# Output products on 64 rows in turns, small products placed later, parts handed over by halves

## The chip, the cores and the metric

One core of one Trainium2 chip runs the whole program. The metric is the device time of one execution in microseconds. The kernel is written directly for the engines: TensorE (PE, with its weight loads as PEld), VectorE (DVE), ScalarE (ACT), GpSimd (POOL) and SyncE (SP), which issues the DMAs. Each engine has its own program, and they meet in semaphores.

## The reference

The input x is 16 samples of 128 channels, 32x32 pixels, f32. Four residual layers follow one another, each `x = x + layer(groupnorm(x))`, with a group norm over 4 channels:

- Layer 0: a convolution gives three maps (two offsets, one mask) for each pixel; the normalised image is sampled bilinearly there, and then comes a depthwise 3x3 and a pointwise convolution.
- Layer 1: the image is pooled 3x3; a 3x3 convolution of the pooled image gives 18 offsets and 9 masks; the pooled image is sampled at nine places for each pixel (deformable convolution) and multiplied with 9 x 128 x 128 weights.
- Layer 2: a dense 3x3 convolution with weights made from `weight` and `r_matrix`.
- Layer 3: a 1x1 projection to two halves of 64 channels. One goes through a small two-layer net (x_conv), the other through a horizontal and a vertical strip attention (attn). Both are gated, concatenated and go through the output projection:

```python
out = jnp.concatenate([spatial_map, channel_map], axis=1)   # 64 + 64 channels
return _pw(out, proj_out_w, proj_out_b)                      # 128 -> 128
```

## The kernel before

All is f32. A pass takes two samples, so there are eight passes: a loop of seven (`PASSES - 1`), in which the next pass's first layer is worked in, and a last one without it. In layers 0 to 2 a sample's 128 channels lie on the 128 partitions. In layer 3 the two samples share the partitions, 64 channels each (sample 0 on 0 to 63, sample 1 on 64 to 127). A call of matmul (`mm`) in f32 stands as two records in the trace, each with its weight load. A product of 512 columns is a half image of one sample.

The order of TensorE's work is written out by hand. `conv` (L516) makes a 3x3 convolution as 9 products for the upper half (h = 0) and 9 for the lower half (h = 1), and takes hooks: `hooks[h, k]` is called before product (h, k). In a pass TensorE does this:

1. Layer 1's offset parts of sample 0: `offset_parts(2, ...)` (L488), 18 products of 32 output columns in turns on four column groups, into the bank psO. ScalarE's `parts` (L932 is the copy that many helpers share) moves them to SBUF as two copies, one for each half of the image, and `offsets(i, 2, 27)` (L500) sums the four groups for each of 8 tiles, 16 records. VectorE adds the bias (L1528); TensorE doubles the result (`doubles`, L602); VectorE makes hat functions from it (`hats`, L1502 to L1514). Then the same parts for sample 1 (`offset_parts(3, ...)`), a far test, block transposes (L594), `offsets(i, 3, 27)`.
2. For each sample the sampling products (`near`, L627: 64 rows by 144 columns, in turns on two row groups), which ScalarE copies out, and layer 1's convolution from the samples (`conv(psO[0], w1, ...)`). In the second of these convolutions hooks hold, for the next pass: at (0, 3) layer 0's tap rows (`tap_rows`, L641), at (1, 3) layer 0's small offset products (`next_offsets`: `offsets(i + 1, 0, 6)`, L500, 16 records of 54 rows and 6 columns), and at (1, 6) the product of layer 0's far test (`start_far`, L649). Between rows and offsets the rows go to ScalarE (`rows`), through nine DMAs that shift them (SP, `move`), and back to ScalarE (`tap_tiles`, two copies).
3. Layer 2's convolution (`conv(psO[1], w2, ...)`, L516), with layer 0's block products of the next pass between its products (L558, L564, L576). Before that stands, at (0, 5), the group mean of "L2B" (L479).
4. Layer 3 in pieces (L847 to L866), with the next pass's pointwise and depthwise convolution (`conv0`, L720) as filling between them; at the end the output products (L901, L902): for sample s and half h one with the spatial map (`sm`, weights `woT[:, s, 0, :]`) and one with the channel map (`at`, weights `wo2[:, s, :]`), both over 128 rows. The weights have zeros on the other sample's 64 rows. The group mean of "L1B" stands before sample 1's second half.

VectorE's order in the same places: after layer 1's sampling it takes the convolution of each sample into x (L1612), makes statistics (L1225 to L1233), waits for the group mean, and makes the affine (L1246 to L1262; a step on GpSimd, L455, in between). For sample 1 it does, ahead of the wait for the convolution, the next pass's layer 0: the offsets' sum (`start_offsets`, L1332, L1299, L1303), the flag (`start_flag`, L1309, L1343) and seven steps of the hat functions of sample 0 (`start_hat`, L1352 to L1369). At the end of a pass it does: pooling of sample 0 (`pool3`, L1387 to L1393) with the residual of layer 0 in between (L1398), the variance of "L1B", the last residual of sample 0 (`store_ready`, L1737), the scale of "L1B" for ScalarE's normalisation (L954), pooling of sample 1, the last residual of sample 1.

## Time and profile before

| | |
|---|---|
| median of 3 runs | 1719.94 us (1717.85 to 1722.87) |
| the profiled execution | 1719.42 us, span 1717.6 us |
| TensorE busy | 1591.8 us, 93% of the span |
| VectorE, ScalarE busy | 66%, 38% |
| mean granted clock of TensorE | 0.958 |
| a pass in the loop | about 203 us |

A row of the timeline merges equal instructions that follow one another; its length runs from the first one's start to the last one's end, and the ends of matmuls are modelled. "idle [.. <- ..]" is how long the engine did nothing before it, and what ended that. A window's mean clock of 0.75 means that half of it was at 1.2 GHz.

### The profile page before, as it was taken

The numbers are of one execution on the slowest core, as the hardware profiler recorded it, in microseconds if no ns is written. First come the engines' busy times: TensorE is split into PE (matmuls) and PEld (weight loads), VectorE is DVE, ScalarE is ACT, GpSimd is POOL, SyncE is SP. The second block draws the span as 40 slices with busy tenths as digits, with TensorE's granted clock in tenths as the row PEclk, the third lists the DMA queues.
The fourth block names the chain that finished last, engine by engine and source line by source line (L and its number), as shares of the span: only waits on it lengthen the run. The fifth ranks groups of instructions, "written<-read, shape, count | busy, mean of one in ns | idle before, by whom it ended". The sixth has DMA issues, their size and how long they took to land.

```text
span 1717.6 us, 22494 instructions
## 1 busy us (share of the span) xinstructions
PE 1591.8 (93%) x7252; PEld 837.6 (49%) x7252; DVE 1141.4 (66%) x2139; ACT 659.3 (38%) x1066; POOL 50.2 (3%) x76
## 2 busy tenths in 40 slices
PE   2979999999999999999999999999999999999975
PEld 1537453565435554365534645355543655337422
DVE  4358349864598457883498835985469844887266
ACT  2126224461345413453244622555134541346131
POOL 2000000000000000000000000000000000000000
PEclk8989999999999999999999999999999999999987
DMA  3000000100001000000001000010000100000000
GB/s 117 14 13 2 7 1 1 51 5 4 1 1 52 7 2 1 26 27 7 1 1 51 2 6 1 1 52 7 2 1 14 39 7 2 1 25 2 1 0 25
DMA packets 7971, 24.61 MB, mean 14 GB/s; under 512 B 1664, under 2 KB 2368, under 8 KB 7792
## 3 DMA queue, kind: packets, MB, share of 16 engines
q1 hardware_dynamic: 7792, 22.40, 3.5%
q8 instruction: 91, 1.49, 0.4%
q14 instruction: 88, 0.72, 0.1%
HBM read 12.13 MB, written 8.39 MB: 12 GB/s over the span
## 4 chain that ended last, share of the span: by engine, by line
PE 75%; DVE 11%; issue 6%; ACT 4%; SPq 3%; DMA 1%; POOL 1%; DVEq 0%; POOLq 0%; ACTq 0%
PE psN L516 14%; PE psO L516 13%; PE psN L851 11%; PE psO L720 7%; PE psN L720 5%; PE psN L627 4%; PE psO L576 4%; SPq L414 3%; ACT samp L932 2%; DVE samp L1662 2%; PE psN L594 2%; PE psN L558 2%; PE psN L564 2%; PE psM L500 2%; PE psN L901 1%
## 5 line engine op out<-in xcount | busy, mean ns | idle before, releaser
L516 PE MATMUL psO<-samp,w 128*128 128x512 f32 x576 | 285.2, 631 | 0.0
L516 PE MATMUL psN<-xn,w 128*128 128x512 f32 x576 | 278.7, 605 | 1.7 <-DVE yout L1409 0.9
L1143 ACT ACTIVATE samp<-psN,vec 128x512 f32<-128x512 f32 x160 | 110.0, 687 | 130.4 <-PE psN L851 130.4
L516 PEld LDWEIGHTS psO<-samp,w 128*128 128x128 f32 x576 | 106.6, 200 | 102.6 <-issue 96.2
L1317 DVE COPY xblk<-psN 120x256 f32<-120x256 f32 x128 | 54.3, 424 | 142.7 <-PE psN L558 142.7
L932 ACT ACTIVATE samp<-psN 128x576 f32<-128x576 f32 x192 | 118.2, 676 | 58.1 <-PE psN L627 58.0
L516 PEld LDWEIGHTS psN<-xn,w 128*128 128x128 f32 x576 | 98.3, 189 | 84.5 <-issue 84.5
L932 ACT ACTIVATE G<-psN 120x256 f32<-120x256 f32 x128 | 49.1, 383 | 229.6 <-PE psN L564 229.6
L720 PE MATMUL psN<-img,w 128*128 128x512 f32 x288 | 133.4, 608 | 0.0
L720 PE MATMUL psO<-img,w 128*128 128x512 f32 x288 | 133.0, 603 | 0.0
L627 PE MATMUL psN<-GQt,xq 64*128 64x144 f32 x1536 | 123.1, 297 | 10.6 <-ACT samp L932 9.0
L627 PEld LDWEIGHTS psN<-GQt,xq 64*128 64x128 f32 x1536 | 103.3, 186 | 26.1 <-ACT samp L932 16.5
L954 ACT ACTIVATE xn<-x,gst 128x1024 f32<-128x1024 f32 x32 | 40.1, 1254 | 189.7 <-DVE gst L1262 189.7
L1587 DVE TENSOR_TENSOR GTs<-hf 128x576 f32<-128x576 f32 x128 | 95.7, 758 | 15.1 <-DVE flag L1309 11.8
L1598 DVE STREAM_TRANSPOSE GQt<-GTs 128x576 f32<-128x576 f32 x128 | 96.9, 767 | 3.9 <-PE psN L627 3.9
L455 POOL TENSOR_TENSOR gst<-gst,neg_half 128x1 f32<-128x1 f32 x64 | 42.4, 662 | 1588.7 <-DVE gst L1251 1588.7
L720 PEld LDWEIGHTS psO<-img,w 128*128 128x128 f32 x288 | 53.7, 188 | 68.4 <-issue 68.4
L851 PE MATMUL psN<-samp,kh_w 128*128 128x512 f32 x160 | 79.1, 636 | 8.3 <-DVE samp L1662 8.3
L720 PEld LDWEIGHTS psN<-img,w 128*128 128x128 f32 x288 | 51.9, 188 | 69.8 <-issue 69.8
L851 PE MATMUL psN<-samp,kv_w 128*128 128x512 f32 x160 | 78.6, 633 | 5.8 <-DVE samp L1662 5.8
L500 PE MATMUL psM<-tab,Gd 128*128 128x27 f32 (+1 forms) x384 | 51.8, 280 | 33.0 <-ACT Gd L932 33.0
L576 PE MATMUL psO<-G,xblk 120*128 120x128 f32 x512 | 79.7, 278 | 0.9
(156 smaller groups left out, 2299.9 us busy)
## 6 DMA issues: line engine op xcount, KB each, us to landing
xin<-in_x SPq DMA_DIRECT2D x16, 512.0 KB, 4.1
out<-yout SPq DMA_DIRECT2D x16, 512.0 KB, 3.7
pool_v<-rows SPq DMA_DIRECT2D x72, 25.5 KB
w<-in_w SPq DMA_DIRECT2D x2, 576.0 KB, 5.1
samp<-in_r SPq DMA_DIRECT2D x1, 576.0 KB, 6.8
tab<-in_tab SPq DMA_DIRECT2D x1, 513.0 KB, 5.3
kh_w<-in_kh SPq DMA_DIRECT2D x1, 320.0 KB, 5.4
kv_w<-in_kv SPq DMA_DIRECT2D x1, 320.0 KB, 5.6
```

The lines of the kernel that those rows point to most:

```text
L414: sp.dma_start(pool_v[k:k + ROWS - K9 + 1:K9].rearrange("p r c -> p (r c)"), rows[k:k + ROWS - K9 + 1:K9, first:first + H * EDGE])\
L500: last = mm(ps[s][:, 4 + m * t:4 + m * t + m], off_parts[s][0:used, C * t:C * t + C], table, start=True, stop=True)
L516: last = mm(dst[:, h, :], wgt[:, k, :], rhs(h, k), start=(k == 0), stop=(k == K9 - 1))
L576: last = mm(psO[0][:, p // 4, C * (p % 4):C * (p % 4) + C], xblk[p % 2][:, u, :], G1[p % 2][:, u, :], start=(u == 0), stop=(u == 1))
L627: last = mm(pair(s, u)[:, g, :].rearrange("p (k r c) -> p k r c", k=K9, c=SW)[:, :, :, cols], xQ[rows, t, a, e, :], w[rows, e, :, :, cols] ...
L720: ins = mm(dst[:, h, :], w0[:, k, :], window(img[s])(h, k), start=(k == 0), stop=(k == K9 - 1))
L851: mm(product(m), lhsT, rhs[:, HALF * h:HALF * h + HALF], start=True, stop=True)\
L932: return nc.scalar.activation(out, in_, ACT.Copy)
L1143: nc.scalar.activation(out, bank(m)[0:out.shape[0]], fn, **kw).then_inc(l3_act.sem, 1)
L1317: v_.tensor_copy(xblk[b][:].rearrange("p h c -> p (h c)"), psT[0:BLK, 1, 0:2 * C])\
L1587: v_.tensor_tensor(GQ[n % 2][:].rearrange("p (k a b) -> p k a b", a=QR, b=QB), hy[:, ORDER[n]].unsqueeze(3).broadcast_to((C, PAIRS * K9, Q ...
L1598: v_.transpose(GQt[o % RING][:].rearrange("p e k r c -> p (e k r c)"), GQ[(n - 1) % 2][:])\
```

## The change

Four edits:

- The output products are made on 64 rows each. For each half, first the spatial and then the channel map, and within these the two samples in turns, sample 0 on partitions 0 to 63 and sample 1 on 64 to 127. The four accumulations go to the same four banks as before. The wait for `added(i + 1, 1)` stands before all of them and the group mean of "L1B" behind all of them. Both samples' semaphore increments come in the last pair of products.
- `next_offsets` moves from (1, 3) to (1, 6), `start_far` from (1, 6) to (1, 8).
- `offset_parts` counts its semaphore once for each half, `parts` on ScalarE waits and counts for each half, and `offsets` takes the tiles of the upper half (0, 2, 4, 6) first and then waits for the lower half. `tap_tiles`, which also feeds `offsets`, still counts once.
- VectorE's seven steps `start_hat(own, i + 1, 0, part)` move from ahead of the wait for the second sample's convolution to behind its statistics, ahead of the affine of "L2B".

```diff
@@ offset_parts, in the loop over h
-                last.then_inc(parts_product.sem, 1)
+                    last.then_inc(parts_product.sem, 1)
@@ offsets
-                pe.wait_ge(parts_ready.sem, parts_ready.at(i, max(n, 1)))
-                for t in range(TILES):
+                for t in (0, 2, 4, 6, 1, 3, 5, 7):
+                    if t < 2:
+                        pe.wait_ge(parts_ready.sem, parts_ready.at(i, (1, 2 * n - 2 + t)[n > 0]))
@@ hooks of layer 1's second convolution
-                            hooks[1, 3] = next_offsets
-                            hooks[1, 6] = lambda: start_far(i + 1)
+                            hooks[1, 6] = next_offsets
+                            hooks[1, 8] = lambda: start_far(i + 1)
@@ layer 3's output products
-                for s in range(2):
-                    if s and more:
-                        pe.wait_ge(added.sem, added.at(i + 1, 1))
-                    for h in range(2):
-                        hh = slice(HALF * h, HALF * h + HALF)
-                        if h and more and s:
-                            group_mean(i, "L1B", order)
-                        mm(final[s][:, h, :], woT[:, s, 0, :], sm[:, hh], start=True, stop=False)
-                        last = mm(final[s][:, h, :], wo2[:, s, :], at[:, hh], start=False, stop=True)
-                    last.then_inc(l3_product.sem, 1)
+                if more:
+                    pe.wait_ge(added.sem, added.at(i + 1, 1))
+                for h in range(2):
+                    hh = slice(HALF * h, HALF * h + HALF)
+                    for m, weights, maps in ((0, woT[:, :, 0, :], sm), (1, wo2, at)):
+                        for s in range(2):
+                            own = slice(C2 * s, C2 * s + C2)
+                            last = mm(final[s][:, h, :], weights[own, s, :], maps[own, hh], start=(m == 0), stop=(m == 1))
+                            if h and m:
+                                last.then_inc(l3_product.sem, 1)
+                if more:
+                    group_mean(i, "L1B", order)
@@ parts, on ScalarE
-                act.wait_ge(parts_product.sem, parts_product.at(i, n - 1))
                 for b in range(2):
-                    last = copy(...)
-                last.then_inc(parts_ready.sem, 1)
+                    act.wait_ge(parts_product.sem, parts_product.at(i, 2 * n - 3 + b))
+                    copy(...).then_inc(parts_ready.sem, 1)
@@ VectorE, for sample s of layer 1
                     if s and more:
                         start_offsets(own, i + 1)
                         start_flag(own, i + 1)
-                        for part in range(START_HAT):
-                            start_hat(own, i + 1, 0, part)
 
                     dve.wait_ge(conv_ready.sem, conv_ready.at(i, 3 + s))
                     ...
                     stats(own, ("L2A", "L2B")[s], order)
+                    if s and more:
+                        for part in range(START_HAT):
+                            start_hat(own, i + 1, 0, part)
                     affine(own, ("L2A", "L2B")[s], order)
```

## Rows read from the trace of the kernel before

**Rows 1.** The page, part 1: busy us (share of the span) and instructions of each engine.

```profile
PE 1591.8 (93%) x7252; PEld 837.6 (49%) x7252; DVE 1141.4 (66%) x2139; ACT 659.3 (38%) x1066; POOL 50.2 (3%) x76
```

**Rows 2.** Timeline, 787 to 804 us: start, us, engine, line, operation, out<-in, count [idle before].

```profile
787.93 6.25 PE L516 MATMUL psO<-samp,w 128*128 128x512 f32 x14
...
794.89 1.15 ACT L932 ACTIVATE Gd<-pool_v 54x512 f32<-54x512 f32 x2 [3.83 <-DMA pool_v<-rows]
...
796.10 2.32 PE L500 MATMUL psM<-tab,Gd 54*128 54x6 f32 x16 [1.91 <-ACT Gd L932]
...
798.35 5.49 PE L516 MATMUL psO<-samp,w 128*128 128x512 f32 x6
...
803.63 0.42 PE L649 MATMUL psM<-flagf,tab 128*128 128x1 f32 x2
...
803.92 3.02 PE L516 MATMUL psO<-samp,w 128*128 128x512 f32 x6
```

**Rows 3.** Windows: length, busy us of PE, PEld, DVE, ACT, POOL, then PEclk, DMA.

```profile
183.98:196.69 12.71, 10.81 (x31) 6.48 (x31) 2.85 (x11) 1.46 (x4) 0.00 (x0) 0.73 0.01 2
...
sum 84.27, PE 70.89 PEld 40.43 DVE 20.32 ACT 10.21 POOL 0.00; mean PE 10.13 PEld 5.78 DVE 2.90 ACT 1.46 POOL 0.00
...
738.90:740.76 1.86, 1.86 (x20) 1.82 (x18) 1.83 (x4) 1.33 (x3) 0.00 (x0) 1.00 0.00 0
...
1704.00:1709.00 5.00, 5.00 (x7) 2.00 (x6) 0.00 (x0) 0.00 (x0) 0.00 (x0) 0.51 0.00 0
```

**Rows 4.** Timeline of layer 1's offset products, second sample.

```profile
738.89 1.87 PE L500 MATMUL psM<-tab,Gd 128*128 128x27 f32 x16
```

**Rows 5.** Timeline behind them, 804 to 818 us: VectorE, and TensorE's first block product.

```profile
804.35 0.19 DVE L1352 SCALAR_TENSOR_TENSOR om_start<-om_start,tab 128x32 f32<-128x32 f32 x1
...
807.10 0.42 DVE L1369 SCALAR_TENSOR_TENSOR hat<-hat,mk 128x256 f32<-128x256 f32 x1
...
812.95 0.21 DVE L1262 TENSOR_SCALAR gst<-gst 128x1 f32<-128x1 f32 x1
...
817.02 0.38 PE L558 MATMUL psN<-ident,strip 128*120 128x128 f32 x2
```

**Rows 6.** Timeline from one pass to the next, 711 to 728 us.

```profile
711.44 1.02 PE L901 MATMUL psN<-samp,woT 128*128 128x512 f32 x2
...
715.57 1.23 DVE L1393 TENSOR_TENSOR img<-img,pool_v 128x1024 f32<-128x1024 f32 x1
...
719.09 1.26 ACT L954 ACTIVATE xn<-x,gst 128x1024 f32<-128x1024 f32 x1 [3.84 <-DVE gst L1262]
...
719.22 4.63 PE L488 MATMUL psO<-img,w1off 128*32 128x512 f32 x36 [0.53 <-issue]
...
725.03 1.97 PE L500 MATMUL psM<-tab,Gd 128*128 128x27 f32 x16 [1.18 <-ACT Gd L932]
...
725.51 1.28 DVE L1737 SCALAR_TENSOR_TENSOR yout<-psN,vec,yout 128x1024 f32<-128x1024 f32 x1
...
727.57 0.38 DVE L1528 TENSOR_TENSOR om<-psM,offb 128x216 f32<-128x216 f32 x1 [0.78 <-PE psM L500]
```

**Rows 7.** The chain: a step before the offsets' sum, and an earlier doubling product.

```profile
726.78 0.67 issue
...
321.71 1.81 PE psM L602 x4
```

**Rows 8.** Timeline of TensorE, the sampling products of sample 1.

```profile
772.03 1.25 PE L627 MATMUL psN<-GQt,xq 64*128 64x144 f32 x16
```

**Rows 9.** Timeline of the first pass, VectorE's sum of the offsets.

```profile
117.25 0.38 DVE L1528 TENSOR_TENSOR om<-psM,offb 128x216 f32<-128x216 f32 x1 [1.53 <-PE psM L500]
```

**Rows 10.** Timeline of the last pass's end.

```profile
1703.34 2.08 PE L901 MATMUL psN<-samp,woT 128*128 128x512 f32 x2 [2.21 <-DVE xq L1732]
...
1709.81 1.28 DVE L1737 SCALAR_TENSOR_TENSOR yout<-psN,vec,yout 128x1024 f32<-128x1024 f32 x1 [6.52 <-PE psN L902]
...
1713.24 1.28 DVE L1737 SCALAR_TENSOR_TENSOR yout<-psN,vec,yout 128x1024 f32<-128x1024 f32 x1 [2.15 <-PE psN L902]
```

More of the change, by code:

```diff
@@ L260, in conv_preact_kernel @@
         strip8_ready = signal("strip8_ready", 2)
-        parts_product = signal("parts_product", 2)
+        parts_product = signal("parts_product", 4)
         rows_product = signal("rows_product", 1)
         rows_ready = signal("rows_ready", 1)
-        parts_ready = signal("parts_ready", 3)
+        parts_ready = signal("parts_ready", 5)
         xT_product = signal("xT_product", 2)
@@ L973, in parts @@
                 s = n % 2
-                act.wait_ge(parts_product.sem, parts_product.at(i, n - 1))
                 for b in range(2):
-                    last = copy(off_parts[s].rearrange("p (j b r c) -> p j b r c", b=2, j=STRIPS, c=SW)[:, :, b],
-                                psO[s][:, b, :].rearrange("p (r j c) -> p j r c", j=STRIPS, c=SW))
-                last.then_inc(parts_ready.sem, 1)
+                    act.wait_ge(parts_product.sem, parts_product.at(i, 2 * n - 3 + b))
+                    copy(off_parts[s].rearrange("p (j b r c) -> p j b r c", b=2, j=STRIPS, c=SW)[:, :, b],
+                         psO[s][:, b, :].rearrange("p (r j c) -> p j r c", j=STRIPS, c=SW)).then_inc(parts_ready.sem, 1)
             def tap_rows(j):
```

## The prediction

> **What bounds the kernel now.** I read the page first: TensorE is busy for 93% of the span, the next one for 66% [rows 1]. So an edit pays where TensorE itself waits, or where it works at half clock. The page's clock line is coarse, so I went through one pass of two samples (the stretch 690 to 905 us) in the timeline and asked for the granted clock in short windows. The reader is to see two places in a pass where TensorE isn't streaming at 2.4 GHz. One lies in layer 1's second convolution, where the small products of layer 0's offsets stand: TensorE's last row product ends at 794.0, the offsets begin at 796.10, when ScalarE's copy has ended (794.89 + 1.15 = 796.04), and the six records after them take 5.49 us [rows 2]. A full-clock record takes (6.25 - 0.60) / 13 = 0.435 us by the row of 14 ahead of it, so six should take 2.6: the clock had fallen to 1.2 GHz after the wait and the small products. The other lies between the passes, where layer 3's output products end, layer 1's offset parts run and the kernel waits for VectorE [rows 6, 7].
>
> **Offsets three products later, the flag two later.** I cut the same stretch out of each of the seven passes that have it: from the end of product (1, 2) to the end of the convolution. The seven take 84.27 us; the first has a granted clock of 0.73, which is 12.71 x 0.27 x 2 = 6.9 us at half speed [rows 3]. (Four are like it, three have 0.85.) What lies in such a stretch if nothing waits and the clock stays up: six products of two records, 12 x 0.43 = 5.16; the 16 small records, 1.9, which is what 16 others take at full clock [rows 4]; the flag's product, 0.29 from its start at 803.63 to the next one's at 803.92 [rows 2]. Sum 7.35, seven times 51.5. So 84.3 - 51.5 = 32.8 us are there to be had, 2.05 x 7 = 14.4 of waiting and 18.4 of half clock.
> Does the wait go? The copies end 796.04 - 794.0 = 2.04 us behind the old place; three products are 3 x 0.86 = 2.58. Everything ahead of the copies (the row product at (0, 3), ScalarE's copy, nine DMA issues on SP, the landing) hangs on a product that isn't moved, so 0.5 us of slack remain. Does the clock stay? Then only 1.9 us of small products stand between dense ones, in place of 4. The offsets of layer 1's second sample are 16 such records between transposes and the sampling products; the granted clock over them is 1.00 [rows 3, 4], and so it is at all eight of their places. I take it that the clock stays up. The bounds of this edit: 14.4 gained (only the wait goes) and 32.8.
> The flag's product is now two products (1.72) behind the offsets; VectorE needs some 0.8 for the sum, the maximum and the comparison in between, so it doesn't wait. But it ends only 0.9 us ahead of the convolution, and the seven steps of the hat functions behind it run 804.35 to 807.52 = 3.2 us [rows 5]. In their old place they would now hold x's sum and the statistics until about 3 us behind the convolution, and TensorE's group mean, five products into the next one, would wait almost 2 us. Their move behind the statistics is what hides that. Its price stands on VectorE: now the affine ends at 813.16, which is 6.4 behind the convolution's end at 806.8 (803.92 + 3.02 less the 0.16 of a record's tail), and layer 0's first block product comes at 817.02, 10.2 behind [rows 5]. With x's sum at once and the hats in between, the affine ends 1.8 later, at 8.2, two products of hats are out at 9.4, ScalarE's normalisation at 9.5. That is within 10.2: nothing, with 0.8 us of slack; without it each us late would cost seven.
>
> **The output products on 64 rows.** Eight products of 16 records, 711.44 to about 718.7 with a group mean: 6.9 us at 0.43 a record [rows 6]. A record of 64 rows can run beside one on the other row group: the sampling products (64x144, in turns on the groups) take 1.25 / 16 = 0.078 us each [rows 8], where 144 of 512 columns alone would be 0.43 x 144 / 512 = 0.12, and the last one's tail is in the 1.25. So about half: 16 x 0.215 + 0.43 = 3.9 us. From both sides: 3.9 and, without overlap, 6.9.
> Every pass but the last goes on into the next one, and there VectorE decides. Its row is unbroken: the pooling of sample 0 ends at 716.80, the affine, the residual of sample 0, ScalarE's normalisation, the four pooling steps of sample 1, the residual of sample 1 from 725.51 to 726.79, then 0.67 us of loop end, and only then the sum of layer 1's offsets at 727.57, for which TensorE's offsets have been done since 727.0 [rows 6, 7]. The row of 727.57 names those offsets as what ended its wait of 0.78, but the last of them was 0.57 us old by then. Of that chain only the group mean of L1B comes earlier; VectorE, busy with the pooling until 716.80, takes it from TensorE's product at 716.90, so that is under 0.1 us, say 0.06. TensorE itself will start the parts at about 717.0 in place of 719.22 and then wait longer for VectorE. The 3.0 us aren't seen in seven of the eight ends of a pass: 0.06 x 7 = 0.4 gained.
> At the end of the last pass they are. There the products start at 1703.34 (VectorE's weights), the two residuals at 1709.81 and 1713.24 [rows 10]. The clock is 0.51 from 1704 to 1709 [rows 3] and full behind that. On two row groups 16 records take 8.5 turns of 0.86 at half clock; 5.5 us give 6.5 turns, the other two 0.43 each at full clock, end near 1709.8. The residuals follow one another, 1709.8 and 1711.1: 2.0 us gained (0 if the groups don't overlap, 2.4 at most).
> The Trainium skill, TensorEngine Tiling (Array Packing), under Tiling Modes, says that a change of tiling mode drains the array. That speaks against the edit: 128-row products stand on either side. By a record's 0.59 us against its spacing of 0.43 a drain is 0.16 us, two a pass; all but the last pass have VectorE as cover, so the sum would be 0.3 us higher. No row here shows a drain by itself.
>
> **Layer 1's parts by halves.** ScalarE copies the first half while TensorE makes the second, and four of the eight offset products go ahead. In the passes behind another one ScalarE isn't free before 719.09 + 1.26 = 720.35 [rows 6] and the offsets end near 723.4 in place of 727.0, but VectorE takes them at 727.57 as before: nothing. In the first pass VectorE did wait for them, 1.53 us until 117.25 [rows 9]; half a copy (0.55) and four products (0.5) less, 1.2 us gained. The second sample's offsets stand behind the block transposes on TensorE: nothing.
> A cost of the first and second edit together: TensorE is now empty from about 721.6 until VectorE lets it go at 728.0, 1.5 to 2.5 us longer. The clock falls earlier. In five of the seven places it already fell before the doubling products (321.71: 1.81 us for four, against 1.0 at full clock) [rows 7]; in the other two they now take 0.8 more: 0.8 x 2 = 1.6 lost at most; I take 0.8, since the times against the gate shift anyway. The parts of sample 1, whose first 3 to 4 us run at half clock in each pass already, keep that.
>
> **Sum**, against the profiled execution (1719.4 us, 0.5 below the median of the runs shown): 32.8 + 0.4 + 2.0 + 1.2 - 0.8 = 35.6. I take 1 us off for one pass in which the clock falls all the same. 1719.4 - 34.6 = 1684.8; I say 1685. Its own range is 1680 to 1691: the clock's phase in the last pass, which is at half clock for long stretches, is open by 2 to 3 us, and one or two passes may keep the low clock.
>
> **Rivals.**
> (a) The wait goes, the clock still falls at the offsets. For: the small products are there still, and they keep TensorE almost empty for 1.9 us. Against: the clock over the 16 like records [rows 3]. Then 14.4 + 2.8 = 17.2 are gained: 1702.
> (b) The row groups don't overlap (both samples' banks or weight loads get in each other's way). For: these products accumulate in pairs on each bank, which the sampling products don't. Against: rows 8. It costs only the 2.0 of the end: 1687.
> (c) TensorE's saved time does come through, because the loop end of VectorE isn't its own work but waits for something of TensorE's. For: the row of 727.57 names TensorE's offsets [rows 6]. Against: they had ended, and the chain has 0.67 us without a releaser there [rows 7]. At most 0.7 x 7 = 5 more: 1680.
> (d) Slower: the clock gate. Shorter products, a longer wait and narrow parts let the clock fall before the parts of sample 0 and stay down until the block transposes. The parts of sample 1 would take 9.2 in place of 6.0, the parts of sample 0 4.6 more, of which VectorE's cover hides all but 0.8, the doubling 0.3 more: 4.3 x 7 = 30 lost. If it falls at the offsets too, gained are only the 17.2 of (a): 1732. It decides from 5 us lost in each pass if (a) doesn't hold, 2.5 if it does. Against: the idle time ahead of the parts, 715.6 to 717.0, is shorter than the wait of 2.05 that together with 1.9 us of small products made the clock fall.
>
> **Chances.** The forecast 0.73, (a) 0.12, (b) 0.06, (c) 0.04, (d) 0.05. A measurement of this kernel tells about 0.3% (5 us) from no change. All but (d) are faster by more: faster 0.94, the same 0.02 (a mild (d)), slower 0.04. Ranges: low end 1679 with (c); above, the forecast's own range and half of the way to (a), and (a) itself to 1702: 1679 to 1702.
>
> **What would show it.** Right: the seven stretches from product (1, 2) to the convolution's end at 7.4 us with a granted clock of 1.00; no wait of the small offsets for ScalarE; x's sum right at the convolution's end; layer 0's first block product still 10 us behind it; output products of 3.9 us; the sum of layer 1's offsets unmoved, 16.1 us behind their start, with TensorE waiting some 4 us before it. Wrong: a clock of 0.5 behind the offsets (then (a)); block products that wait for VectorE's hats; parts of sample 0 that take over 4.7 us (then (d)).

## The result: 1677.95 us, and the profile after

The changed kernel takes 1677.95 us (1677.09 to 1678.53, 4 runs), beside it the kernel before 1719.64 us: ratio 0.9755, 95% interval 0.9738 to 0.9772. That is 41.7 us less where 34.6 were forecast, 7 us under the forecast and 1 us below the range. The profiled execution is 1677.09 us, span 1675.3, so the spans stand 42.3 apart. One execution of x_fill, further down, ran at a granted clock of 0.556 from start to end (2659.68 us); it is left out of that experiment's median and ratio.

Part 1 of the page of the kernel after, as [rows 1]:

```profile
PE 1549.2 (92%) x7252; PEld 823.7 (49%) x7252; DVE 1140.2 (68%) x2139; ACT 662.8 (40%) x1066; POOL 50.2 (3%) x76
```

The instructions are the same in number and VectorE's work is unchanged; TensorE is busy for 42.6 us less. Its idle time is as long as before (span less busy time: 126.1 and 125.8 us): what it no longer waits at the small products it now waits at the ends of the passes. Where the gain lies, stretch by stretch, over both profiled executions ("the end of the sampling products" is the start of their last record):

| stretch (us, before, after) | before | after | moved | forecast |
|---|---|---|---|---|
| first pass: parts of sample 0 to the end of its sampling products | 33.52 | 32.12 | -1.4 | -1.2 |
| seven ends of a pass: output products' start to the end of the next pass's first sampling products | 281.50 | 278.12 | -3.4 | +0.4 |
| seven times: end of sample 1's sampling products to layer 2's convolution | 174.91 | 142.77 | -32.1 | -32.8 |
| seven times: layer 2's convolution to `conv0` | 329.71 | 327.50 | -2.2 | 0 |
| last output products to the end | 14.29 | 11.11 | -3.2 | -2.0 |
| the rest | | | 0.0 | 0 |
| set off for the clock | | | | +1.0 |

The small offsets in the kernel after, the same place as [rows 2, 5] (timeline; the columns are those of [rows 2]):

```profile
777.02 1.15 ACT L936 ACTIVATE Gd<-pool_v 54x512 f32<-54x512 f32 x2 [3.83 <-DMA pool_v<-rows]
...
778.82 1.95 PE L502 MATMUL psM<-tab,Gd 54*128 54x6 f32 x16
...
780.70 1.98 PE L518 MATMUL psO<-samp,w 128*128 128x512 f32 x4
...
782.52 0.28 PE L651 MATMUL psM<-flagf,tab 128*128 128x1 f32 x2
...
783.60 4.57 PE L518 MATMUL psN<-xn,w 128*128 128x512 f32 x10
783.80 1.28 DVE L1613 SCALAR_TENSOR_TENSOR x<-psO,vec,x 128x1024 f32<-128x1024 f32 x1 [0.74 <-PE psO L518]
...
793.50 0.38 PE L560 MATMUL psN<-ident,strip 128*120 128x128 f32 x2
```

The copies end at 778.17, 0.65 ahead of the offsets, which no longer wait. The products behind them run at 2.4 GHz (four records in 1.98, where six took 5.49 in [rows 2]), x's sum begins 0.2 behind the convolution's end, and the first block product comes 9.90 behind layer 2's start. From one pass to the next, as [rows 6]:

```profile
693.06 1.13 PE L903 MATMUL psN<-samp,woT 64*128 64x512 f32 x4
694.03 1.02 PE L903 MATMUL psN<-at,xq 64*128 64x512 f32 x4
...
696.82 0.38 PE L479 MATMUL psM<-gst,tab 128*128 128x2 f32 x2
697.11 1.23 DVE L1396 TENSOR_TENSOR img<-img,pool_v 128x1024 f32<-128x1024 f32 x1
700.70 7.07 PE L488 MATMUL psO<-img,w1off 128*32 128x512 f32 x36 [3.49 <-issue]
...
707.70 1.97 PE L502 MATMUL psM<-tab,Gd 128*128 128x27 f32 x16
709.70 0.38 DVE L1531 TENSOR_TENSOR om<-psM,offb 128x216 f32<-128x216 f32 x1 [1.58 <-PE psM L502]
710.14 1.00 PE L604 MATMUL psM<-om,tab 128*128 128x216 f32 x4 [0.47 <-DVE om L1531]
711.07 4.62 PE L488 MATMUL psN<-img,w1off 128*32 128x512 f32 x36
...
721.96 1.41 PE L629 MATMUL psN<-GQt,xq 64*128 64x144 f32 x16 [0.71 <-DVE GQt L1601]
```

Four things are to be seen. The products are 3.55 us long in place of 7.09 (from the first record's start to the last one's end, less that one's tail of 0.16; some 0.2 of the 7.09 is the group mean that stood among them). The parts of sample 0 begin at 700.70, 7.64 behind the products' start, although the image they read was ready at 698.34: almost nothing of the 3.5 us has come through. Those parts take 7.07 us, mostly at the low clock. And the doubling products (1.00) and the parts of sample 1 (4.62) run at 2.4 GHz. At five of the seven ends of a pass it is so (parts of sample 0: 6.24 to 7.07 us). At the other two the parts of sample 0 take 4.6, and those of sample 1 have the low clock (6.79 and 5.77). The same stretch by granted clock (windows; columns as [rows 3]) of the kernel after, parts of sample 0, then the offsets' sum to the parts' end:

```profile
700.70:706.94 6.24, 6.24 (x34) 1.59 (x36) 5.05 (x5) 1.58 (x2) 0.00 (x0) 0.59 0.25 91
...
709.70:715.70 6.00, 5.56 (x41) 1.88 (x41) 5.04 (x10) 1.74 (x4) 0.00 (x0) 1.00 0.46 157
```

and of the kernel before, the two parts:

```profile
719.22:723.85 4.63, 4.62 (x36) 1.27 (x36) 3.33 (x3) 1.13 (x1) 0.00 (x0) 1.00 0.32 120
...
728.93:735.19 6.26, 6.26 (x38) 1.61 (x37) 5.91 (x9) 0.42 (x2) 0.00 (x0) 0.73 0.46 137
```

The stretch at 1.2 GHz has moved from sample 1's parts to sample 0's.

What holds the parts back stands in no row of the timeline but "issue". The rows of TensorE's branches do show it: at the loop's end, `COMPARE_BRANCH` (duration in ns, least/median/most, then the first and last start), after:

```profile
L928 PEldq COMPARE_BRANCH  x7: 83/3377/3617, 301.9 to 1488.9; - x7
```

and before:

```profile
L924 PEldq COMPARE_BRANCH  x7: 83/3549/3761, 308.9 to 1527.0; - x7
```

One such branch costs TensorE's sequencer (the part of an engine that issues its instructions) some 3.5 us. It stands behind the group mean of "L1B" in the queue, so it can begin only when that mean's statistics are there: at this end of a pass 3.85 us behind the products' start (before: 3.97). It took 3.52 there, and the parts began 0.27 later, 7.64. So it is at all six ends where the branch jumps back: the parts begin 0.25 to 0.27 behind its end, in the kernel before as well (0.26 to 0.33), though their image is ready at 5.27 (before: 5.36). Before, the queued products covered all but 0.4 to 0.7 us of the branch; now nothing does. Into the last pass the loop doesn't jump: there the branch took 0.083, and the parts begin 5.41 behind the products.

The DMA packets in the trace show what a jump waits for. In each of these six branches a packet of the kind "instruction" (16 KB, queue 8) begins 0.92 to 0.99 us behind the branch's start and takes 0.88 to 1.20; the next instruction of TensorE's queue comes 1.38 to 1.56 behind the packet's end. The branch that doesn't jump has no such packet.

### The profile page after: what moved, and what is told of

Read it like the earlier page. It is cut to its first block, busy times and chain, and to the rows that moved or that the text cites. A ratio compares the mean times of both kernels' runs of the same rounds, so it can differ in the third digit from the quotient of the medians.

```text
span 1675.3 us, 22543 instructions
## 1 busy us (share of the span) xinstructions
PE 1549.2 (92%) x7252; PEld 823.7 (49%) x7252; DVE 1140.2 (68%) x2139; ACT 662.8 (40%) x1066; POOL 50.2 (3%) x76
## 4 chain that ended last, share of the span: by engine, by line
PE 76%; DVE 13%; issue 6%; ACT 3%; POOL 1%; DVEq 0%; SPq 0%; DMA 0%; POOLq 0%; ACTq 0%
PE psO L518 15%; PE psN L518 15%; PE psN L853 11%; PE psO L722 8%; PE psN L722 5%; PE psN L629 5%; PE psO L578 4%; DVE samp L1666 2%; PE psN L596 2%; PE psN L566 2%; PE psN L560 2%; ACT samp L936 2%; PE psO L488 2%; PE psM L502 2%; DVE GQt L1601 1%
## 5 line engine op out<-in xcount | busy, mean ns | idle before, releaser
L518 PE MATMUL psO<-samp,w 128*128 128x512 f32 x576 | 270.2, 603 | 0.0
L518 PEld LDWEIGHTS psO<-samp,w 128*128 128x128 f32 x576 | 101.2, 190 | 95.3 <-issue 88.8
L629 PE MATMUL psN<-GQt,xq 64*128 64x144 f32 x1536 | 128.2, 306 | 12.7 <-ACT samp L936 7.1
L629 PEld LDWEIGHTS psN<-GQt,xq 64*128 64x128 f32 x1536 | 109.7, 196 | 26.6 <-ACT samp L936 12.6
L488 PE MATMUL psO<-img,w1off 128*32 128x512 f32 x288 | 47.8, 774 | 29.5 <-issue 20.5
```

Of the source, the lines that this page charges most:

```text
L488: last = mm(dst[32 * g:32 * g + 32, h, :], w[:, k, :], window(src)(h, k), start=(k < 4), stop=(k >= K9 - 4), skip_group_check=True)
L518: last = mm(dst[:, h, :], wgt[:, k, :], rhs(h, k), start=(k == 0), stop=(k == K9 - 1))
L629: last = mm(pair(s, u)[:, g, :].rearrange("p (k r c) -> p k r c", k=K9, c=SW)[:, :, :, cols], xQ[rows, t, a, e, :], w[rows, e, :, :, cols] ...
```

## Experiments: the parts of the change alone

The first four undo or do one part of the change; their edits are hunks of the diff shown above.

**b_rows**: the kernel before with the fourth hunk alone.

```diff
+                    for m, weights, maps in ((0, woT[:, :, 0, :], sm), (1, wo2, at)):
+                        for s in range(2):
+                            last = mm(final[s][:, h, :], weights[own, s, :], maps[own, hh], ...)
```

> The kernel before with the 64-row output products alone (offsets, flag, hats and parts as before). Theory G (the gate): the products end after 3.55 us in place of 7.1, TensorE's branch at the loop's end (3.5 us, it begins only when the wait of the group mean of L1B is over) is no longer covered by products, the low clock falls on sample 0's parts, which VectorE's chain covers, and sample 1's parts run at 2.4 GHz: about 3.4 us over the seven ends of a pass and 3 to 4 at the end of the last pass, 6 to 8 us less: 1712 to 1714. Rival V (the record's reckoning: VectorE covers everything but the last pass's end, the clock stays as it was): 0.4 + 2.0 - 0.8 = 1.6 us less: 1718. Sample 1's parts: 4.6 us in most passes (G) or 5.2 to 6.7 (V).

Measured 1720.91 us (12 runs) beside 1720.23, ratio 0.9999 (0.9981 to 1.0017): no change, where my theory had a gain of 6 to 8. Its timeline at the end of a pass:

```profile
711.42 1.13 PE L901 MATMUL psN<-samp,woT 64*128 64x512 f32 x4
...
718.87 6.25 PE L488 MATMUL psO<-img,w1off 128*32 128x512 f32 x36 [3.31 <-issue]
...
725.17 1.08 ACT L934 ACTIVATE Gd<-psO 128x512 f32<-128x512 f32 x2 [5.13 <-PE psO L488]
...
728.31 0.38 DVE L1530 TENSOR_TENSOR om<-psM,offb 128x216 f32<-128x216 f32 x1 [1.83 <-PE psM L500]
```

The parts of sample 0 are slow and ScalarE's copies both come behind them, so the offsets' sum (om) begins 16.9 behind the products, now waiting for TensorE and not at 16.1. The seven ends of a pass are 285.24 us (+3.7), the end of the last pass 3.4 shorter. Sample 1's parts have the full clock at three of the seven ends (4.6 us) and take 5.5 to 5.7 at the others. In this profile the stretch to layer 2, which the edit leaves alone, is 4.9 shorter, since the low clock behind the small products was shorter in more of the passes; so much can lie between two profiles where the clock falls differently.

**b_hooks**: before with the hooks at (1, 6) and (1, 8) and the hat steps behind the statistics.

```diff
+                            hooks[1, 6] = next_offsets
+                            hooks[1, 8] = lambda: start_far(i + 1)
```

> The kernel before with the offsets at (1, 6), the flag at (1, 8) and the hats behind the statistics, nothing else. If this part is worth what the trace of the changed kernel says (32.2 us in the second convolutions, 2.2 between layer 2's start and the first block product): 34.4 less, 1685. Theory G says nothing more; if the parts at the pass's start need the 64-row products to get the full clock, sample 1's parts stay at 5.2 to 6.7 us here. Rival (the shifted phase of the clock gate alone put the low clock elsewhere): they take 4.6 here as well and the time is 1679 to 1681.

Measured 1682.32 us (5 runs), ratio 0.9779 (0.976 to 0.9798): 37.9 of the 41.7 us. The two stretches of the middle are 142.77 and 327.50, the same as in the full change; the ends of a pass are 282.09, as before (281.50).

**b_halves**: before with the counting and copying by halves alone.

```diff
+                for t in (0, 2, 4, 6, 1, 3, 5, 7):
+                    if t < 2:
+                        pe.wait_ge(parts_ready.sem, ...)
```

> The kernel before with layer 1's parts handed over by halves alone. Reckoned: 1.2 us less from the first pass, nothing in the others, since VectorE takes the offsets' sum when its own chain is through: 1718.5. Theory G: the tiles of the upper half go ahead, so TensorE is empty longer before the doubling products and the clock falls earlier, which leaves sample 1's parts at 5.2 to 6.7 us. Rival: the halves are what moved the low clock; then sample 1's parts take 4.6 and 3 to 5 us go: 1715.

Measured 1714.24 us (8 runs), ratio 0.9973 (0.9955 to 0.9991). The first pass gives 1.2, the ends of a pass nothing (281.38 for 281.50). The end of the last pass is 11.56 for 14.29 with the same old products: in this run they have the full clock there, in the profile of before [rows 3, 10] half. So those 2.7 us come from where the low clock happened to fall, not from the edit. Over 8 runs the median is 6.0 lower than before, clear of noise; the edit's own stretches show 1.3 of it, and where the rest comes from stays open. The rival has failed: sample 1's parts take 5.3 to 6.6 us at six of the seven ends.

**a_nohats**: the changed kernel with the seven hat steps back in front of the wait for the convolution.

```diff
                         start_flag(own, i + 1)
+                        for part in range(START_HAT):
+                            start_hat(own, i + 1, 0, part)
```

> The changed kernel with the seven hat steps back ahead of the wait for the second convolution. Reckoned: x's sum comes about 3 us behind the convolution's end, the group mean of L2B on TensorE 2 us late, and TensorE's branch into layer 0 (3.5 us, it begins when that group mean's wait is over) as much later: 2 to 3.5 us in each of seven passes, 14 to 25 us more than the changed kernel: 1692 to 1703. Rival: TensorE's branch and the group mean are covered by the products that are queued; then under 3 us more: 1678 to 1681.

Measured 1692.19 us (4 runs), ratio 0.9837 (0.9818 to 0.9857), 14.2 slower than the full change. Layer 2 to `conv0` is 342.66 us, +15.2, 2.17 a pass. Its timeline:

```profile
791.82 4.57 PE L518 MATMUL psN<-xn,w 128*128 128x512 f32 x10
...
794.52 1.28 DVE L1615 SCALAR_TENSOR_TENSOR x<-psO,vec,x 128x1024 f32<-128x1024 f32 x1
...
797.80 0.38 PE L479 MATMUL psM<-gst,tab 128*128 128x2 f32 x2 [1.42 <-DVE gst L1236]
...
803.75 0.38 PE L560 MATMUL psN<-ident,strip 128*120 128x128 f32 x2
```

x's sum comes 2.7 behind layer 2's start in place of 0.2, the group mean waits 1.42, and the first block product is at 11.93 in place of 9.90. The branch ahead of it (L673, median 3.6 us) stands behind the group mean of "L2B" in TensorE's queue, as the loop's stands behind "L1B": the later the mean, the later the branch. The traces bear this out pass by pass (us behind layer 2's start): the branch begins 0.62 to 0.65 behind the last instruction of the statistics, and in all seven passes of this run, and in all seven of the kernel before, the first block product comes 1.92 to 1.93 behind the branch's end. In the kernel before the branch ends at 8.02 to 8.55 and the block product comes at 9.95 to 10.47; here at 9.94 to 10.35, and 11.86 to 12.27. In the full change it ends at 7.37 to 7.87, TensorE's records follow one another without a break, and the block product has its 9.90 from the products ahead of it.

**a_nohalves**: the changed kernel without the halves.

```diff
-                    last.then_inc(parts_product.sem, 1)
+                last.then_inc(parts_product.sem, 1)
```

> The changed kernel with layer 1's parts handed over whole again, as before. Theory B: TensorE's branch at the loop's end and the low clock put the end of sample 0's parts at 13.8 us behind the output products' start; whole copies then take 3.2 us to VectorE's sum in place of 1.94, which is 0.7 to 0.9 a pass behind VectorE's own readiness, and the first pass loses its 1.2: 6 to 8 us more than the changed kernel, 1684 to 1686, the same as without the 64-row products (1682.3). Rival (the edits are worth what each was worth alone, 64-row products 0, halves 5): 1683. Rival (VectorE covers the halves in all passes but the first, as in the record): 1679. Tells theory B from the record's reckoning; the row to read is the sum of the offsets, 16.7 to 17 or 15.9 behind the products' start.

Measured 1688.87 us (5 runs), ratio 0.9835 (0.9809 to 0.986): 10.9 slower than the full change. The ends of a pass are 288.66 (+10.5), the first pass +1.5. The timeline of the same place as above:

```profile
698.61 1.13 PE L901 MATMUL psN<-samp,woT 64*128 64x512 f32 x4
...
706.59 6.26 PE L488 MATMUL psO<-img,w1off 128*32 128x512 f32 x36 [3.83 <-issue]
...
716.03 0.38 DVE L1530 TENSOR_TENSOR om<-psM,offb 128x216 f32<-128x216 f32 x1 [2.37 <-PE psM L500]
```

The sum begins 17.42 behind the products, where it comes at 16.64 at this end of the full change, and VectorE waits 2.37 for TensorE. Over the six ends with a jump the mean is 17.7 for 16.0. Halves are worth nothing between passes while the parts of sample 0 are fast (b_halves), and 1.5 us a pass once the 64-row products have made them slow.

## Experiments: what delays the parts, and what the clock does

**x_head**: the changed kernel with the group mean of "L1B" at the head of the next pass, behind the branch.

```diff
-                if more:
-                    group_mean(i, "L1B", order)
@@ head of one_pass
+                group_mean(i, "L1B", FIRST)
                 pe.wait_ge(added.sem, added.at(i, 2))
```

> The changed kernel with the group mean of L1B moved from the end of a pass to the head of the next, so that TensorE's branch at the loop's end isn't behind its wait. Theory B (the branch of 3.5 us, begun when the group mean's wait is over, sets the start of sample 0's parts at 7.6 us behind the output products' start, and what falls to half clock is these parts): the parts start at 5.5 and take 4.6, the sum of the offsets stays at about 16.0 (VectorE), the low clock goes back to the doubling and to sample 1's parts (5.2 to 6.7 us), and the seven ends of a pass take about 3 us more in all: 1681. Rival (the branch costs time on the path): 1 us less in each, 1671. Rival (the start of the parts waits for something else): they stay at 7.6, 1678.

Measured 1679.66 us (5 runs), ratio 0.9776 (0.9754 to 0.9798): 1.7 slower by the medians, 3.1 by the spans of the profiled executions, though the intervals of the ratios overlap. Its timeline:

```profile
700.10 4.63 PE L488 MATMUL psO<-img,w1off 128*32 128x512 f32 x36 [1.18 <-DVE img L1394]
...
710.77 0.38 DVE L1529 TENSOR_TENSOR om<-psM,offb 128x216 f32<-128x216 f32 x1 [0.94 <-issue]
711.21 1.80 PE L604 MATMUL psM<-om,tab 128*128 128x216 f32 x4 [2.92 <-DVE om L1529]
712.95 6.20 PE L488 MATMUL psN<-img,w1off 128*32 128x512 f32 x36
```

The parts begin 5.33 behind the products' start (694.77), when their image is ready, and run at full clock: the branch was what held them. (It now begins 0.12 us behind the products' start and is over at 3.4 to 4.0.) But the sum stays at 16.0, bound by VectorE; TensorE then waits 2.92 for it, and the doubling (1.80) and the parts of sample 1 (6.20) have the low clock. The ends of a pass take 281.12, 3.0 more than in the full change. The late, slow parts of sample 0 are what the full change gains from.

**x_head_y1**: x_head, and VectorE does sample 1's last residual ahead of its pooling.

```diff
                 store_ready(1)
+                if more:
+                    for part in range(4):
+                        pool3(own, 1, part, i, order)
```

> As x_head, and the residual of sample 1 (1.28 us) on VectorE stands ahead of sample 1's pooling, in the 1.39 us in which VectorE waits for ScalarE's normalisation. Theory B: VectorE's chain to the sum of the offsets is 1.1 to 1.3 us shorter (14.8 behind the products' start), but doubling and parts run at half clock, TensorE sets the start of sampling (about 28.6), and 0.3 us a pass are left: 1676. Rival (VectorE's chain alone decides): 1.2 us in each of seven, 1670. Rival (nothing, another wait takes the residual's place): 1681, as x_head.

Measured 1686.31 us (5 runs), ratio 0.9817 (0.9793 to 0.9841): 6.6 slower than x_head, where the sum should have come earlier. The chain of waits in it (start, length, what):

```profile
708.99 0.06 DVEq L1786
709.04 4.15 issue
713.20 0.06 DVEq L1786
```

VectorE's last pooling step (1.23 us) starts at 708.90, the sum comes at 713.30, and between them lies the jump at the end of VectorE's loop: the branch's own record is 0.06 us long, and the first instruction behind it comes 4.15 later. In the kernel before the same jump runs from 724.56 to 727.46, 2.9 us, so the 0.67 us of [rows 7] was only the part of it that stuck out from under the last residual. The DMA issues of this run show what else changed: the next samples' loads went out at 708.68, as the branch began, where x_head has them at 713.71. Below are these issues, and then what moved between 709.0 and 713.2 (queue, kind: packets, MB, share of the 16 DMA engines).

```profile
703.46 1.84 SPq L420 DMA_DIRECT2D out<-yout  x2
708.68 0.97 SPq L428 DMA_DIRECT2D xin<-in_x  x2
...
q1 hardware_dynamic: 286, 1.04, 69.9%
q14 instruction: 1, 0.01, 0.5%
```

**x_late_load**: x_head_y1 with those loads waiting for the doubled offsets.

```diff
-                        sp.wait_ge(added.sem, added.at(i, s + 1))
+                        sp.wait_ge(doubled_ready.sem, doubled_ready.at(i, 1))
```

> As x_head_y1, but SP issues the loads of the next x only when sample 0's doubling products are made, in place of when the last x is summed. There the sum of the offsets came at 17.0 behind the products' start although VectorE's work was done 1.3 us earlier; its branch at 12.7 was followed by the next instruction only at 16.9 (3.05 us in x_head, 4.2 here). Theory L (earlier stores let the 512 KB loads go out at 12.4, ahead of the 8 KB of code that VectorE's branch needs): the branch takes 3.1 us again, the sum comes at 15.8, the time is that of x_head: 1679.5. Rival (the branch is longer because nothing is queued ahead of it any more): it stays at 17.0, 1686.

Measured 1677.89 us (4 runs), ratio 0.977 (0.974 to 0.98), 8.4 faster than x_head_y1. Chain of waits:

```profile
706.00 0.06 DVEq L1786
706.05 2.69 issue
708.74 0.06 DVEq L1786
```

With the loads out of its way the same jump takes 2.69 in place of 4.15, and the sum is back at 15.6. In this jump (706.0 to 708.74) the one instruction packet is the only thing that moved:

```profile
q14 instruction: 1, 0.01, 1.1%
```

The packets' times tell the two apart. Here the 8 KB packet begins 0.98 to 1.01 us behind the branch at the six jumps, in x_head_y1, among 1 MB of loads, 2.00 to 2.42 behind it; its own length (0.3 to 0.5) and the time from its end to the next instruction (1.3 to 1.5) are about the same in both. So the jump waits for its code, and the loads delay the start of that packet by 1.0 to 1.4 us.

**x_fill**: x_head_y1 with three products that nothing reads between the offsets and the doubling.

```diff
+                for _ in range(3):
+                    mm(psO[1][:, 0, :], w1[:, 0, :], window(img[0])(0, 4), start=True, stop=True)
                 doubles(i, 0)
```

> As x_head_y1, and while TensorE would wait for VectorE's sum of the offsets it makes three 128x512 products that nobody reads (they go to the bank that sample 1's parts overwrite). Theory B with the clock: doubling 0.93 and sample 1's parts 4.6 us, TensorE is ready before VectorE, sampling starts 27.1 behind the products' start in place of 28.1 in the changed kernel: 1 us in each of seven less, the first pass 2 us more: 1672. Rival (the clock of these parts isn't worth anything on the path): as x_head_y1, 1676 or, by the three products' own 2.6 us, slower than it.

Measured 1689.48 us (5 runs), ratio 0.9829 (0.9806 to 0.9853), 3.2 slower than x_head_y1. Timeline of TensorE:

```profile
713.44 4.54 PE L748 MATMUL psN<-img,w 128*128 128x512 f32 x6
717.82 0.89 PE L604 MATMUL psM<-om,tab 128*128 128x216 f32 x4
718.64 4.64 PE L488 MATMUL psN<-img,w1off 128*32 128x512 f32 x36
```

The filling itself ran at the low clock (six records in 4.54) and brought it back for what follows, 4.64 us of parts at full clock, but cost more than that: the first pass is 2.5 us longer, the seven ends 1.3.

**x_head_fill**: x_head with two such products ahead of the offsets and three behind.

```diff
                 offset_parts(2, img[0], w1off)
+                for _ in range(2):
+                    mm(psO[1][:, 0, :], w1[:, 0, :], window(img[0])(0, 4), start=True, stop=True)
                 offsets(i, 2, 27)
+                for _ in range(3): ...
```

> As x_head (group mean of L1B at the head of a pass), with two unread 128x512 products ahead of the offsets of sample 0 and three behind them. Theory K (the low clock comes from TensorE's empty stretch before the doubling products): the clock stays at 1.00 there, doubling 0.93, sample 1's parts 4.6 in all passes, sampling starts 28.0 behind the products' start (VectorE: 12.2 behind its sum) and ends 0.5 earlier than in the changed kernel; seven times 0.4 to 0.5 gained, 2 to 4 lost in the first pass: 1677 to 1680. Against x_head 0 to 3 less. Rival (filling products change nothing in the clock): as x_head plus the products' own time, 1682 and over.

Measured 1677.56 us (5 runs), ratio 0.9778 (0.9752 to 0.9805). Timeline:

```profile
712.07 0.38 DVE L1532 TENSOR_TENSOR om<-psM,offb 128x216 f32<-128x216 f32 x1 [0.66 <-issue]
...
713.43 4.62 PE L488 MATMUL psN<-img,w1off 128*32 128x512 f32 x36
...
724.33 1.25 PE L629 MATMUL psN<-GQt,xq 64*128 64x144 f32 x16 [0.71 <-DVE GQt L1602]
```

Now both samples' parts have 2.4 GHz, and the ends of a pass take 275.96, 2.2 less than in the full change. The sampling products start 12.26 behind the sum, and so they do in the full change (721.96 - 709.70): this is VectorE's chain of hats and transposes, and past it the clock can give nothing more here. The first pass pays 3.5 us for the filling, so the whole is even.

The last two go to the hooks of the middle. **d_14**: the changed kernel with the small offsets at (1, 4).

```diff
-                            hooks[1, 6] = next_offsets
+                            hooks[1, 4] = next_offsets
```

> The changed kernel with layer 0's small offset products at (1, 4) in place of (1, 6): one product behind the old place. The wait for ScalarE's copies is 2.04 - 0.86 = 1.2 us in each of seven passes, 8.3 in all. Theory E (wait and small products together make the clock fall): 1.2 of wait and 1.9 of small products are 3.1 us of an almost empty TensorE, the clock falls in some passes and not in others, 3 to 8 us more: 1689 to 1694. Rival (only the wait makes it fall, and 1.2 is short of that): 1686. Rival (the small products alone are harmless only at (1, 6)): low clock in all seven, 1700 and over.

Measured 1699.77 us (4 runs), ratio 0.9896 (0.987 to 0.9922). The stretch to layer 2 is 162.46 us for 142.77, +19.7, in 7 passes: 1.18 x 7 = 8.3 of waiting (the idle time of 1.05 and the tail of the record ahead of it), 11.4 at the low clock. Its ends of a pass are those of the full change in code, but 281.12 us, 3.0 more: the parts of sample 0 were slow at six of them, 7.1 to 7.4 us at five.

```profile
786.41 1.95 PE L502 MATMUL psM<-tab,Gd 54*128 54x6 f32 x16 [1.05 <-ACT Gd L936]
788.29 5.40 PE L518 MATMUL psO<-samp,w 128*128 128x512 f32 x8
```

A wait of one us ahead of the small products was enough for the clock to fall behind them (8 records in 5.40 in place of 3.6), in all seven passes, where my theory had it in some. That it is the wait and not the place (1, 4) isn't separated: no run has the small products there without a wait.

**d_twice**: the changed kernel with the 16 small records made twice, at (1, 6) and without a wait.

```diff
+                    for t in range(TILES):
+                        mm(ps[0][:, 4 + 6 * t:4 + 6 * t + 6], off_parts[0][0:ROWS, ...], tab[...], ...)
                     offsets(i + 1, 0, 6)
```

> The changed kernel with layer 0's 16 small records at (1, 6) made twice, 32 in a row, without a wait. Their own time is 1.95 x 7 = 13.7: 1691.6. Theory S (54-row, 6-column records leave TensorE as good as empty for the clock gate): 3.9 us of them are as long as wait and products together were before, the clock falls in all or nearly all seven passes and the products behind run at half clock for 3 to 5 us, 1.5 to 2.5 lost in each: 1702 to 1709. Rival (only waiting makes it fall): granted clock 1.00 over the stretch, 1691.6.

Measured 1700.62 us (4 runs), ratio 0.9905 (0.9874 to 0.9935). The stretch is 166.85, +24.1: at the one place where the clock stayed up it is 1.79 longer, so 12.5 are the added records (the forecast had 13.7) and 11.6 the low clock, which fell in six of the seven places with no wait at all.

## Why the prediction was wrong, and where it was right

Right: the term that carries it. The hooks' stretch moved by 32.1 for 32.8, all seven passes, no wait and a clock of 1.00. d_14, with half of the wait left, has the low clock in all seven passes, and d_twice, with twice the small products and no wait, in six; a_nohats leaves this stretch as it is and loses 15.2 of the gain in the next one, which is what moving the hats was for. Right too are the overlap of the row groups (3.55 us for the 3.9 reckoned; four records begin every 0.86 us) and the first pass (1.4 for 1.2). Accumulating in pairs on each bank, the reason of rival (b), hindered nothing. By the Trainium skill, TensorEngine Tiling (Array Packing), Tiling Modes, the switch of mode drains the array; the trace agrees that the switch costs something: at all seven ends the first record on 64 rows begins 0.53 behind the last one on 128 rows, for 0.44 otherwise, and the first four records take 0.97 to the next, for 0.86. That is 0.2 us at this switch, for the 0.16 estimated.

The step that failed is the account of the end of a pass: "TensorE itself will start the parts at about 717.0 in place of 719.22", "The clock falls earlier ... in the other two they now take 0.8 more", and "The parts of sample 1, whose first 3 to 4 us run at half clock in each pass already, keep that". It gave +0.4 us over the seven; measured are -3.4. The parts did not start earlier, since the branch behind the group mean holds them (x_head shows that: without that order they start 2.3 earlier). The reckoning had put that branch, some 3.5 us, at nothing; the idle 0.53 "<-issue" ahead of the parts in [rows 6] was its end. The 3.5 us that the shorter products freed became an idle time ahead of the parts of sample 0, 3.49 where (d) had reckoned 1.4 (715.6 to 717.0). There the clock fell, one stretch earlier than before, and those parts lie under VectorE's cover, as long as the copies go by halves (a_nohalves: without them 10.5 lost). In return the doubling and the parts of sample 1 have the full clock in six of the eight passes: those parts take 35.6 us in the seven for 42.2. Part of these 6.6 us is given back, since VectorE's chain of 12.25 from the sum to the sampling products binds next. So between passes the first edit alone costs 3.7 us (b_rows), the third alone gives nothing (b_halves), and with the second in place the two together gain 3.4. That 3.4 is not a fixed price: three more runs have the same code at the end of a pass, and their seven ends take 279.1 (a_nohats), 278.1 (d_twice) and 281.1 us (d_14), by where the low clock falls. The prediction had the fall of the clock as rival (d), but only as one that stays down over both samples' parts. Its sign for (d), parts of sample 0 over 4.7 us, did come, at five of the seven ends; (d)'s price didn't.

The second miss is "nothing, with 0.8 us of slack" for the hats. Layer 0's block product is not at a fixed 10.2 behind layer 2's start but 9.90 in every pass, for 9.95 to 10.47 before; the seven give the 2.2. The term left out is again a branch, L673 (L671 before). With the hats out of VectorE's way the statistics of "L2B" end at 3.42 behind layer 2's start, for 4.01 to 4.21 before, and the branch begins at 4.04 for 4.63 to 4.84. Before, the block product came 1.92 to 1.93 behind the branch's end in each pass; now the products ahead of it decide. That accounts for all of the 2.2.

Two smaller ones. The last pass's end moved 3.2 for 2.0. With the clock full in both, it is 9.42 us with the new products (a_nohats) and 11.56 with the old (b_halves, b_hooks), so the edit is worth 2.1, for 2.0. The other 1.0 is luck: both profiled executions had the low clock there, the one before for 2.7 us of lost time, the one after for 1.7. And the set-off of 1.0 for a pass that keeps the low clock wasn't needed. Together: 3.8 (-3.4 for +0.4) + 2.2 + 1.2 + 1.0 + 0.2 (first pass) make 8.4, less 0.7 from the hooks' stretch 7.7, by which the spans missed.

Of the rivals, (a) and (b) are out. (c) was right that VectorE's loop end is not its own arithmetic, wrong in what it waits for: it is a jump of some 3 us and the code behind it (x_head_y1, x_late_load), and not TensorE.

Left open: no version that was run beats the full change by more than can be measured; x_late_load and x_head_fill are equal to it. The two weren't run together, nor x_head_fill without filling in the first pass, which by the 2.2 and 3.5 us above could give 2 to 4 us (an estimate). No run has the first and third edit without the second.

## What to carry to other kernels

When work ahead of a wait is shortened, look at what stands in the same queue behind the wait: here a loop branch of 3.4 us lost its cover, and the freed time turned into idle time. Idle time also moves the low clock, and where the low clock lands decides the gain: under another engine's cover it is free, and two edits of which one alone costs time and the other gives nothing can gain together. Read a row "issue" of part of a us at a loop's end as the visible rest of something longer before reordering around it.

## What the runs showed of the hardware

- A jump back at a loop's end cost TensorE 3.3 to 3.8 us in these two kernels (0.083 where it wasn't taken) and VectorE 2.7 to 3.1 us; with two input loads starting as it began it took VectorE 3.8 to 4.2. In each of these jumps a packet of code began 0.9 to 1.3 us behind the branch, or 2.0 to 2.4 among the loads, and the next instruction came 1.3 to 1.6 us behind the packet's end. x_late_load took the loads away, and the packet was early again.
- TensorE's clock fell without any idle time, behind small products: after 32 records of 54x6 in a row (3.73 us) in 6 of 7 places. Behind 16 of them (1.95 us) with no wait it stayed at 2.4 GHz in 7 of 7, and with 1.05 us of idle time ahead of the 16 it fell in 7 of 7.
- Products of 64 rows on the two row groups overlapped fully, also where each bank is accumulated over two of them: 16 records took 3.55 us, where 16 on 128 rows, at 0.43 each, take 6.9. Going over from 128-row to 64-row records cost 0.2 us.
